# Three transfers in flight instead of two in the scatter of tokens into expert slots

## The chip, the cores and the metric

The kernel runs on one core of one Trainium2 chip. The metric is the time of one execution on the device in microseconds. One execution was also recorded by the hardware profiler; its span and its rows are those shown here.

## The reference

One adaLN transformer block for x of shape (4, 512, 256): modulated layer norm, attention with low-rank q and k/v and a rotary part, then modulated layer norm and a mixture of experts. The part that matters here is the mixture of experts. Each of the 2048 tokens goes to 4 of 16 experts:

```python
weights, indices = _gate(xt, gate_w)              # top 4 of 16, from the best 2 of 4 groups
combine = jnp.einsum('tk,tke->te', weights, one_hot(indices, E))
h1 = jnp.einsum('td,eid->tei', xt, W1)
h3 = jnp.einsum('td,eid->tei', xt, W3)
g = silu(h1) * h3 * combine[:, :, None]
y = jnp.einsum('tei,edi->td', g, W2)
z = silu(xt @ Ws1.T) * (xt @ Ws3.T) @ Ws2.T        # shared experts, all tokens
x = x + gb * (y + z)
```

## The kernel before

The work comes in stages. A first stage makes modulations, norms and weights. Attention follows, 64 heads over 256 units, and takes the span up to about 670 us. At its end the second layer norm and the gate's logits are made for the last batch entry.

VectorE then chooses the four experts of every token and computes a slot for each of the 2048 x 4 pairs of token and expert (`places`). Slots are grouped by expert, in 80 tiles of 128 slots (`SLOT_TILES`), padded where an expert's number of tokens is no multiple of 128. Its last step writes `slot_i` and raises `indexed`.

From there two things run side by side. TensorE, VectorE and ScalarE do the two shared experts, 16 positions of one token tile each (`shared_position`); between them VectorE forms the low parts of the routed weights. GpSimd scatters: for each of 16 token tiles and each of 4 ranks, an indirect DMA takes the 128 rows of the tile from SBUF (`h2`, 288 float32 each: 256 values, 16 weights, 16 destinations; 147 KB) and writes them to the DRAM tensor `slots`, each row at its slot number. These are 64 scatters, in the loop over `t` and `r`, line 1913. Before each one but the first two, GpSimd waits until the scatter two before it has landed. Two semaphores, `sent[0]` and `sent[1]`, count the even and the odd scatters by 16.

SyncE waits for `indexed`, starts one weight load (`w2_s`, experts 8 to 12), waits for `listed`, and then for both `sent` semaphores at their final counts:

```python
sp.wait_ge(listed, 1)
for z in range(IN_FLIGHT):
    sp.wait_ge(sent[z], landed(NT * TOPK, z))
sp.wait_ge(z_x, NT)
```

`landed(k, z)` is 16 times the number of scatters among the first k on semaphore z. Only then does SyncE load slot tiles, in order, up to three ahead of the tile being computed (`load_slots`). The routed experts run over these 80 tiles on TensorE, VectorE and ScalarE (`expert_position`), and after each tile GpSimd scatters its 128 result rows to their places in `parts` (line 1926). That loop allows up to four of its scatters in flight, by the four semaphores `e_put`. A last stage adds four parts for each token.

`IN_FLIGHT` is used nowhere else than in the list of semaphores, in `landed`, in SyncE's wait above and in the scatter.

Of the kernel before, what the change touches and what calls it, by code (L numbers as in the profile page):

```python
# [40 lines left out]
NT = NB * TB  # L41
# [7 lines left out]
E, TOPK, EG, TOPG = 16, 4, 4, 2  # L49
# [9 lines left out]
XW = D + 2 * E  # L59
NOWHERE = NT * P * TOPK  # L60
PARTS_AHEAD = 8
IN_FLIGHT = 2
CYCLE = 4
PACK = CYCLE + 2
assert SLOT_TILES % CYCLE == 0 and E ** PACK <= 2 ** 24
# [69 lines left out]
def program(nc, x, cT, wmod, wdn, wqup, wkup, wvup, wout, wrope, trig, eye, qnw_bc, kvw, kvw2, wgate, w13, w2,  # L135
            route, out):
    ctx = ExitStack()
    with ctx:
        def sb(name, shape, dt=F32):
            return ctx.enter_context(nc.sbuf_tensor(name, shape, dt))  # L140

        def sem(name):
            return ctx.enter_context(nc.semaphore(name))
# [6 lines left out]
        slots = nc.dram_tensor("slots", [SLOT_TILES * P, XW], F32).ap()  # L150
# [18 lines left out]
        slot_i = sb("slot_i", [P, NT, TOPK], U32)  # L169
# [139 lines left out]
        h2 = sb("h2", [P, NT, XW])  # L309
# [20 lines left out]
        def rows_of(b):  # L330
# [48 lines left out]
            ("padded", "pad_set", "masked", "listed", "indexed", "extended"))  # L379
        sent = [sem(f"sent{j}") for j in range(IN_FLIGHT)]  # L380

# [83 lines left out]
        def landed(k, z):  # L465

            return 16 * ((k + IN_FLIGHT - 1 - z) // IN_FLIGHT)

# [22 lines left out]
        def _(sp):  # L491
# [131 lines left out]
# [3 lines that stand above are left out]
# [33 lines left out]
        def _(pe):  # L659
# [95 lines left out]
            def aux(t):  # L755
                dst = aux_home(t)
                if AUX_K[t] >= 2:
                    pe.wait_ge(*read_out(AUX_LIST[AUX_K[t] - 2]))
                if t[0] == "pr":
                    _, w, r = t  # L760
                    b, g = r // PAIRS, r % PAIRS
                    if b > 0 and g == 0 and w == 0:
# [11 lines left out]
                elif t[0] == "ht":  # L774
                    _, b, k = t
                    pe.wait_ge(f_xn, b + 1)
                    for q in range(TB):
                        mm = pe.transpose(dst[:, q * P:(q + 1) * P], stage[:, q, k * P:(k + 1) * P], ident[:])
                elif t[0] == "lg":
                    mm = logits(dst[:, 0:TB * E], t[1])  # L780
                elif t[0] == "bt":
                    mm = turn_back(dst, t[2])
                elif t[0] == "ot":
                    p = t[1]

                    pe.wait_ge(s_norm, 2 * p + 2)
                    for q in range(TB):
                        mm = pe.transpose(dst[:, q * P:(q + 1) * P], o_tok[:, p % 2, q, :], ident[:])
                else:
                    _, g, n = t  # L790
                    if n == 0:
                        pe.wait_ge(s_ol, 2 * g + 2)
                    g2 = 2 * g % PAIRS
                    for q in range(2):
                        for pp in range(2):
                            tok = slice((2 * n + q) * P, (2 * n + q + 1) * P)
                            mm = mm3(dst[:, q * D:(q + 1) * D], oT[:, pp, 0, tok], oT[:, pp, 1, tok],
                                     mout[:, 0, g2 + pp, :],
                                     mout[:, 1, g2 + pp, :], pp == 0, pp == 1)
# [985 lines left out]
        def _(pool):  # L1785
# [119 lines left out]
            pool.wait_ge(f_h2, 2 * NB)  # L1905
            pool.wait_ge(extended, 2)
            pool.wait_ge(indexed, 1)
            for t in range(NT):
                for r in range(TOPK):
                    z, landed = r % IN_FLIGHT, (t * TOPK + r) // IN_FLIGHT  # L1910
                    if landed > 0:
                        pool.wait_ge(sent[z], 16 * landed)
                    pool.indirect_dma_start(slots, bass.IndirectOffsetOnAxis(ap=slot_i[:, t, r:r + 1], axis=0),  # L1913
                                            h2[:, t, :], None).then_inc(sent[z], 16)

            last_part = pool.to_reg(NOWHERE - 1)

# [99 lines left out]
```

## Time and profile before

| | us |
|---|---|
| timed executions | 1052.15, 1061.2, 1081.17 |
| median | 1061.2 |
| profiled execution, whole | 1050.47 |
| its span in the trace | 1048.7 |
| TensorE busy | 870.9 (83%) |
| VectorE busy | 733.7 (70%) |
| GpSimd busy | 666.4 (64%) |
| ScalarE busy | 568.5 (54%) |
| GpSimd, 64 scatters into `slots`, busy | 64.2 |
| idle time of GpSimd just before them | 60.3 |

Busy shares are means over stages with different limits, so they don't say what bounds one stage. In the rows, PE is TensorE, PEld its weight loads, DVE VectorE, ACT ScalarE, POOL GpSimd and SP SyncE; L1913 is line 1913 of the kernel. A GpSimd DMA instruction's time is that of the instruction on the engine; its landing is the time from the instruction's start to the moment when all its data has arrived and its semaphore has its full count. The chain that ended last is followed back from the last instruction, at each step to what released it; "issue" in it is time in which nothing that the profile shows was waited for. PEclk is TensorE's granted clock as a share of 2.4 GHz.

### The profile page before, as it was taken

The page shows a single profiled execution, that of the slowest core. Times are in us where ns is not written, and L with a number is a line of the kernel's source. Part 1 is how long each engine was busy: PE and PEld are TensorE (multiplying, and loading weights), DVE is VectorE, ACT ScalarE, POOL GpSimd, SP SyncE. Part 2 cuts the span into 40 slices and gives each one's busy share as a digit, 9 for nine tenths or more (in the row PEclk, how much of TensorE's full clock was granted, in tenths as well). Part 3 has the DMA queues.
Part 4 walks back from the last instruction along what each step waited for, and adds up shares of the span by engine and source line. Part 5 has one row for each costly group of instructions (what it writes and reads, how often), then busy time and mean ns, then how long its engine had stood idle before and what let it go on. Part 6 is the DMA issues. An engine that isn't in the chain of part 4 may idle for free.

```text
span 1048.7 us, 19959 instructions
## 1 busy us (share of the span) xinstructions
PE 870.9 (83%) x6996; PEld 740.5 (71%) x6996; DVE 733.7 (70%) x1648; ACT 568.5 (54%) x1062; POOL 666.4 (64%) x641
## 2 busy tenths in 40 slices
PE   4563799999999999999999997737990899999920
PEld 4552477888878888788888786637880798998920
DVE  5674676878788787978788885586880466666656
ACT  1201387878778788887887886522320344444410
POOL 3513378888888878797888885504666255555544
PEclk9776799999999999999999999857995899999965
DMA  5654243223432233422325135233222333333254
GB/s 183 227 189 95 44 138 80 79 60 68 117 103 58 68 82 84 145 54 74 86 56 159 40 99 211 81 78 92 97 101 108 106 116 110 122 119 119 88 217 184
DMA packets 66332, 113.69 MB, mean 108 GB/s; under 512 B 16981, under 2 KB 43484, under 8 KB 64268
## 3 DMA queue, kind: packets, MB, share of 16 engines
q1 hardware_dynamic: 47337, 71.21, 25.7%
q10 hardware_dynamic: 11987, 23.36, 6.3%
q0 software_dynamic: 6912, 17.84, 4.4%
q8 instruction: 59, 0.97, 0.4%
q14 instruction: 37, 0.30, 0.1%
HBM read 46.45 MB, written 41.68 MB: 84 GB/s over the span
## 4 chain that ended last, share of the span: by engine, by line
PE 59%; DVE 12%; DMA 12%; POOL 7%; issue 5%; ACT 3%; SPq 0%; POOLq 0%; DVEq 0%; ACTq 0%
PE bank L661 13%; PE bank L663 11%; PE bank L662 11%; DMA slots<-h,slot_i 8%; PE bank L834 7%; PE bank L1038 6%; PE bank L811 4%; POOL p_lo L1858 3%; POOL turns L1836 2%; PE bank L1010 2%; PE bank L897 2%; DVE turns L1197 1%; DVE turns L1198 1%; DVE h L1545 1%; DMA rows_f<-turns 1%
## 5 line engine op out<-in xcount | busy, mean ns | idle before, releaser
L1858 POOL TENSOR_TENSOR p_lo<-p_f,p_hi 128x512 f16<-128x512 f32 x256 | 324.5, 1279 | 62.2 <-ACT p_f L1602 61.7
L1224 DVE TENSOR_REDUCE nmax<-bank 128x1 fp32r<-128x512 f32 x256 | 174.3, 686 | 98.1 <-PE bank L811 94.3
L1599 ACT ACTIVATE p_hi<-bank,log_up 128x512 f16<-128x512 f32 x256 | 176.2, 688 | 110.4 <-PE bank L663 101.2
L1602 ACT ACTIVATE p_f<-bank,log_up 128x512 f32<-128x512 f32 x256 | 175.4, 685 | 6.8 <-POOL p_lo L1858 6.8
L834 PEld LDWEIGHTS bank<-vals,p_hi 128*128 128x128 f16 x2048 | 110.4, 98 | 51.3 <-issue 23.6
L834 PE MATMUL bank<-vals,p_hi 128*128 128x66 f16 x2048 | 138.7, 194 | 7.6 <-POOL p_lo L1858 7.0
L661 PE MATMUL bank<-qk 128*128 128x512 f32 x256 | 122.6, 479 | 8.2 <-issue 7.8
L1204 DVE TENSOR_TENSOR qk<-rows_f,qk 128x512 fp32r<-128x512 f32 (+1 forms) x128 | 127.4, 995 | 2.0
L1836 POOL TENSOR_TENSOR turns<-turns 128x512 f32<-128x512 f32 x64 | 89.3, 1398 | 55.1 <-DVE turns L1198 55.1
L834 PE MATMUL bank<-vals,p_lo 128*128 128x66 f16 x1024 | 121.1, 193 | 0.0
L811 PE MATMUL bank<-qk 128*128 128x512 f32 x256 | 103.4, 407 | 6.1 <-DVE nmax L1224 4.0
L1913 POOL DMA_INDIRECT slots<-h,slot_i x64 | 64.2, 1004 | 60.3 <-DMA slots<-h,slot_i 29.6
L663 PE MATMUL bank<-qk 128*128 128x512 f32 x256 | 102.4, 400 | 0.0
L662 PE MATMUL bank<-qk 128*128 128x512 f32 x256 | 101.1, 395 | 0.0
L834 PEld LDWEIGHTS bank<-vals,p_lo 128*128 128x128 f16 x1024 | 96.4, 97 | 0.5
L811 PEld LDWEIGHTS bank<-qk 128*128 128x128 f32 x256 | 79.3, 310 | 19.7 <-DVE nmax L1224 5.1
L1926 POOL DMA_INDIRECT parts<-h,sel_i x80 | 79.7, 997 | 13.2 <-POOL idle L1925 11.7
L1038 PE MATMUL bank<-w_p,gT 88*128 x320 | 82.7, 381 | 0.4 <-DVE gT L1531 0.3
L1591 ACT ACTIVATE qk<-rows_f 128x512 fp32r<-128x512 f32 (+1 forms) x128 | 80.5, 629 | 1.6
L1925 POOL TENSOR_TENSOR idle<-mhalf 128x1 f32<-128x1 f32 x80 | 14.9, 186 | 86.0 <-ACT h L1779 85.9
L1779 ACT ACTIVATE h<-bank 128x256 f32<-128x256 f32 x80 | 30.8, 385 | 62.7 <-PE bank L1038 62.7
L661 PE MATMUL bank<-h_st,wr_hi 128*128 128x512 f32 x128 | 52.5, 410 | 11.5 <-issue 7.3
(231 smaller groups left out, 2106.1 us busy)
## 6 DMA issues: line engine op xcount, KB each, us to landing
rows_f<-turns SPq DMA_DIRECT2D x64, 256.0 KB, 3.9
slots<-pad ACTq DMA_DIRECT2D x4, 2880.0 KB, 10.2
h<-slots SPq DMA_DIRECT2D x80, 144.0 KB, 2.1
w_hi<-parts SPq DMA_DIRECT2D x16, 512.0 KB, 7.8
rows_f<-kl_f SPq DMA_DIRECT2D x32, 192.0 KB, 3.0
w_raw<-in_w ACTq DMA_DIRECT2D x4, 1408.0 KB, 12.1
h_dram<-h_hl SPq DMA_DIRECT2D x3, 1024.0 KB, 4.8
qk<-lat_st SPq DMA_DIRECT2D x16, 192.0 KB, 4.2
```

Source lines behind the costliest of these rows:

```text
L661: pe.matmul(dst, l_hi, r_hi, start=start, stop=False)
L662: pe.matmul(dst, l_hi, r_lo, start=False, stop=False)
L663: return pe.matmul(dst, l_lo, r_hi, start=False, stop=stop)
L811: pe.matmul(max_bank[q % 2][:], qk[:, s % RING, 0, 0, :].rearrange("k (p t) -> k t p", t=TB)[:, q, :], qk[:, s % RING, 1, 0, :], start=Tru ...
L834: mm = pe.matmul(out_bank[s % 2][:, q * VW:(q + 1) * VW], p[:, c, tok], vals[:, s // H * TB + c, a, :], start=(c == 0 and q == 0 and n == ...
L1038: mm = pe.matmul(y_bank[j % 2][:, 0:D], gT[:, j % 2, 0, h, :], w2_s[:, bass.ds(expert, 1), h, :].rearrange("p a n -> p (a n)"), start=(h = ...
L1204: dve.tensor_tensor(qk[rows, s % RING, x, 1, :], rows_f[rows, (s // 2) % 2, x, s % 2, :], qk[rows, s % RING, x, 0, :].bitcast(F32), ALU.su ...
L1224: dve.tensor_reduce(nmax[:, k % MAXES:k % MAXES + 1], max_bank[q % 2][:], AX_X, ALU.max, negate=True)\
L1599: act.activation(p_hi[:, u % TB, :], score_bank[u % 2][:], ACT.Exp, bias=log_up[:, 0:1], scale=SCALE)
L1602: act.activation(p_f[:, u % 2, :], score_bank[u % 2][:], ACT.Exp, bias=log_up[:, 0:1], scale=SCALE)\
L1836: pool.tensor_tensor(turns[:, 0, w], turns[:, 0, w], turns[:, 1, w], ALU.add if w else ALU.subtract).then_inc(s_eo, 1)
L1858: pool.tensor_tensor(p_lo[:, u % TB, :], p_f[:, u % 2, :], p_hi[:, u % TB, :], ALU.subtract).then_inc(s_pl, 1)
```

## The change

Three semaphores instead of two. The scatters are numbered k = 0 to 63 in the same order as before. Scatter k uses semaphore k mod 3 and, from k = 3 on, waits until scatter k - 3 has landed. SyncE waits for three semaphores (counts 22, 21 and 21 times 16) instead of two.

```diff
-IN_FLIGHT = 2
+IN_FLIGHT = 3
...
-            for t in range(NT):
-                for r in range(TOPK):
-                    z, landed = r % IN_FLIGHT, (t * TOPK + r) // IN_FLIGHT
-                    if landed > 0:
-                        pool.wait_ge(sent[z], 16 * landed)
-                    pool.indirect_dma_start(slots, bass.IndirectOffsetOnAxis(ap=slot_i[:, t, r:r + 1], axis=0),
-                                            h2[:, t, :], None).then_inc(sent[z], 16)
+            for k in range(NT * TOPK):
+                t, r = k // TOPK, k % TOPK
+                if k >= IN_FLIGHT:
+                    pool.wait_ge(sent[k % IN_FLIGHT], 16 * (k // IN_FLIGHT))
+                pool.indirect_dma_start(slots, bass.IndirectOffsetOnAxis(ap=slot_i[:, t, r:r + 1], axis=0),
+                                        h2[:, t, :], None).then_inc(sent[k % IN_FLIGHT], 16)
```

## Rows read from the trace of the kernel before

**Rows 1.** Chain that ended last, shares of the span by engine and line.

```profile
PE bank L661 13%; PE bank L663 11%; PE bank L662 11%; DMA slots<-h,slot_i 8%; PE bank L834 7%; PE bank L1038 6%; PE bank L811 4%; POOL p_lo L1858 3%; POOL turns L1836 2%; PE bank L1010 2%; PE bank L897 2%; DVE turns L1197 1%; DVE turns L1198 1%; DVE h L1545 1%; DMA rows_f<-turns 1%
```

**Rows 2.** The chain in order of time: start us, us, what.

```profile
714.56 7.12 DMA slots<-h,slot_i
721.68 0.27 issue
...
754.87 3.67 DMA slots<-h,slot_i
...
772.99 4.32 DMA slots<-h,slot_i
...
810.75 2.45 DMA slots<-h,slot_i
813.33 2.10 DMA h<-slots
815.48 0.70 PE bank L1010 x2
```

**Rows 3.** Timeline, end of the shared experts: start us, us, instruction, idle before.

```profile
784.73 2.83 PE L938 MATMUL bank<-w_p,gT 88*128 88x256 f32 x12
...
788.74 0.42 DVE L1467 TENSOR_TENSOR xa<-xa,zg 128x256 f32<-128x256 f32 x1
```

**Rows 4.** Stretches: length, busy us by engine (instructions), PEclk, DMA share, GB/s.

```profile
790.00:800.00 10.00, 0.00 (x0) 0.00 (x0) 0.00 (x0) 0.00 (x0) 6.83 (x8) 0.56 0.27 106
800.00:810.00 10.00, 0.00 (x0) 0.00 (x0) 0.00 (x0) 0.00 (x0) 7.30 (x8) 0.50 0.30 115
```

**Rows 5.** SyncE's waits: us in total, times, longest us.

```profile
SPq L625 <- DMA slots<-h,slot_i: 99.2, 1, 99.2
```

**Rows 6.** Timeline of GpSimd, the scatter: start us, us, instruction, idle before.

```profile
714.56 1.22 POOL L1913 DMA_INDIRECT slots<-h,slot_i  x1 [27.45 <-DVE slot_i L1408]
716.09 0.96 POOL L1913 DMA_INDIRECT slots<-h,slot_i  x1 [0.30 <-issue]
721.94 0.96 POOL L1913 DMA_INDIRECT slots<-h,slot_i  x1 [4.89 <-DMA slots<-h,slot_i]
723.21 0.96 POOL L1913 DMA_INDIRECT slots<-h,slot_i  x1 [0.30 <-issue]
...
806.59 0.96 POOL L1913 DMA_INDIRECT slots<-h,slot_i  x1 [0.30 <-DMA slots<-h,slot_i]
808.04 0.96 POOL L1913 DMA_INDIRECT slots<-h,slot_i  x1 [0.49 <-DMA slots<-h,slot_i]
```

**Rows 7.** The scatter's line: duration ns min/median/max; what ended the idle before; landing.

```profile
L1913 POOL DMA_INDIRECT slots<-h,slot_i x64: 955/961/1607, 714.6 to 810.8; - x64
...
  DMA slots<-h,slot_i: 29.6, 52
...
DMA to landing us min/median/max: 2.4/2.5/7.1
```

**Rows 8.** TensorE's granted clock by short stretches, columns as in rows 4.

```profile
792.00:793.00 1.00, 0.00 (x0) 0.00 (x0) 0.00 (x0) 0.00 (x0) 0.71 (x1) 0.50 0.19 74
...
822.00:823.00 1.00, 1.00 (x8) 1.00 (x7) 1.00 (x5) 0.38 (x1) 0.00 (x0) 1.00 0.06 21
```

**Rows 9.** Two single scatters: the instruction with its start, and its transfer's landing.

```profile
L1913 POOL DMA_INDIRECT slots<-h,slot_i x1: 959/959/959, 756.3 to 756.3; - x1
...
DMA to landing us min/median/max: 2.6/2.6/2.6
...
L1913 POOL DMA_INDIRECT slots<-h,slot_i x1: 959/959/959, 774.4 to 774.4; - x1
...
DMA to landing us min/median/max: 3.3/3.3/3.3
```

**Rows 10.** The scatter into parts: its line, and its first transfer in the chain.

```profile
L1926 POOL DMA_INDIRECT parts<-h,sel_i x80: 995/997/1013, 825.1 to 1004.6; - x80
...
825.14 4.72 DMA parts<-h,sel_i
```

## Prediction

> **What bounds the kernel now.** I read the chain that ended last first. Its summary gives 8% of the span to the scatter's transfers, `slots<-h,slot_i` [rows 1]; only matrix multiplications take more. The reader should then look at the chain in order of time [rows 2]: from 714.56 to 813.20 us it is nothing but scatter, a transfer of about 2.4 us, 0.27 us of issue, the next transfer. Before it stands VectorE's slot computation, behind it SyncE's first load of a slot tile, which starts at 813.33, and TensorE's first transpose of that tile at 815.48.
>
> Is anything else late at that moment? TensorE's last work of the shared experts starts at 784.73 and lasts 2.83 us, VectorE ends at 789.16 [rows 3]. The table of stretches shows TensorE with no instruction at all from 790 to 810, while GpSimd runs 8 scatters in each 10 us [rows 4]. SyncE waited 99.2 us in one wait for the scatter [rows 5]. So the end of the scatter alone starts the routed experts, and whatever it gains up to about 24 us (813.2 less 789.2) reaches the end, since all 80 tiles are queued behind that load.
>
> What bounds the scatter itself? GpSimd's own timeline [rows 6]: an instruction takes 0.96 us, and where nothing is waited for the next one starts 0.30 us later, a pitch of 1.26 us. The pause of 0.30 stands even before the second instruction, which has no wait in the code, so it isn't the wait's cost. The transfer lands 2.4 to 2.5 us after the start of its instruction (median, [rows 7]). With two in flight, instruction k+2 can start 2.44 + 0.27 = 2.71 us after instruction k. GpSimd alone would need 2.52 for the two. That is the pattern of the last rows: starts 1.45 and 1.26 apart in turn.
>
> **The change part by part.** The third semaphore moves each wait from the transfer two back to the one three back. The number of instructions and bytes stays: 64 scatters of 128 rows. One semaphore is added, the waits on GpSimd go from 62 to 61, and SyncE gets a third wait beside two, all on counts reached at the same moment; I put these at 0.05 us each and so at nothing. GpSimd has only the 64 scatters queued behind the waiting instruction, then the routed experts' steps, which need the loads anyway.
>
> *First stall.* The first transfer lands at 714.56 + 7.12 = 721.68 [rows 2], beside a weight load issued at 713.67. Now scatter 2 (counted from 0) waits for it and scatter 3 follows at 723.21. With three, scatter 2 goes out at 717.35 (716.09 + 0.96 + 0.30) and scatter 3 is the one that waits, until 721.68 + 0.27 = 721.95. Gain 1.26 us; the stall itself stays, since the landing sets it.
>
> *The steady part.* From the start of scatter 3 (723.21) to that of scatter 63 (810.75) are 87.54 us in 60 steps. The instructions' durations in it add up to 60.1 us (the 64.2 of all, less 4.1 for the first three and the last): 60 x 0.96 = 57.6, and the rest in a dozen instructions of up to 1.61 us [rows 7]. The fixed pauses are 60 x 0.30 = 18.0. What remains, 87.54 - 78.1 = 9.4 us, is waiting for landings. With three in flight scatter k+3 can start 2.71 us after scatter k, while GpSimd's own three steps take 3 x 1.26 = 3.78. The wait is met 1.07 us before it is asked, so the steady waiting goes. Late landings stay where they exceed that slack: the one of 4.32 us (started 772.99, [rows 2]) allows the third scatter behind it after 4.32 + 0.27 = 4.59, against 3.8 of own steps, and leaves 0.8. The one of 3.67 (started 754.87) needs 3.94 against 1.26 + 1.26 + 1.49 = 4.0 with its longer neighbour, and leaves nothing. Gain 9.4 - 0.8 = 8.6 us.
>
> *Sum.* 1.3 + 8.6 = 9.9 us. The scatter would end at 803.3 instead of 813.2, still 14 us behind VectorE's last work: next late is the scatter again, now bound by GpSimd's 64 instructions. Behind it nothing depends on absolute time. TensorE's granted clock is 1.00 until 791, 0.60 in the next microsecond and 0.50 from 792 on [rows 8]; its last matmul ended at 787.6. It restarts at 815.48 at 0.50 and has 1.00 from 822. With the scatter ending at 803.3 TensorE restarts at 805.5, after 18 us of idling instead of 28, and by the same rows at 0.50 too; I take the slow start as unchanged.
>
> *Bounds of what the trace doesn't show: three in flight.* The landing of each could grow. I replayed the 64 scatters with their own durations and landings; with two in flight the replay ends at 813.4 (the trace: 813.2), with three at 803.3. With every landing 1.0 us longer the three end at 807, with 1.5 us longer at 815, no gain. I take no lengthening, because of the nearest rows: where a late transfer made them bunch, the transfers started at 754.9 and 756.3 landed after 3.7 and 2.6 us, at 758.6 and 758.9; those started at 773.0 and 774.4 after 4.3 and 3.3, at 777.3 and 777.7 [rows 9]. Two landings 0.3 to 0.4 us apart say that the transfers need far less than 1.26 us each of the engines that move them; so does the DMA share of 0.27 to 0.30 in these stretches [rows 4], some 0.35 us per transfer. On the other side the stretched instructions (2.8 us in all above 0.96) could vanish, which would make the gain 12.7.
>
> The row says 2.44 us from start to landing. The Trainium skill, DMA: Bandwidth & Descriptors, section on the anatomy of one DMA, gives a GpSimd-issued DMA some 2.0 us fixed plus its bytes over 436 GB/s. My estimate from that page is 2.34 us for 147 KB, so two in flight would allow a pitch of (2.34 + 0.27)/2 = 1.31 against 1.26, and the steady gain without late landings would be 3 us, by the measured row (1.355 against 1.26) 5.7. The row is used.
>
> **Against the median.** The profiled execution took 1050.47 us, its span 1048.7 and 1.8 around it; minus 9.9 is 1040.6. The three timed ones are 1052.15, 1061.2 and 1081.17: the profiled one is the fastest of four. From the middle of the four (1056.7) the change gives 1046.8; from the median of three 1051.3. I forecast 1047. A measurement of this kernel can tell about 2% (21 us) from no change, so the forecast, -0.9%, is "within 2%".
>
> **The rivals.**
> *Landings serve in turn.* If the completion of the scatters is the bottleneck, one every 1.35 us, a third in flight only waits longer: every landing grows by 1.36 us, the pitch stays, and only the 1.3 us of the first stall is won: 1049 on the profiled execution, 1055 by the middle of four. For it: every step of the chain is a transfer. Against it: landings 0.3 to 0.4 apart. 10%.
> *Slower: the third overloads the queue.* Place: the 60 steady steps. From a landing of 1.36 us more, 3.8 in all, the three in flight are slower than the two. Rows with such landings exist: the first scatter's 7.12 us beside a load, and the first scatter into `parts`, 4.72 us [rows 10]. At 4.72 the pitch is (4.72 + 0.27)/3 = 1.66, at 7.12 it is 2.46; against 87.54/60 = 1.46 that costs 12 or 60 us: 1063 to 1110 on the profiled execution. The same price comes if GpSimd has no room for a third's descriptors and stands inside its instruction. Against: the scatters into `parts` are 80 with up to four in flight by the code, and their instructions take 995 to 1013 ns, none stretched [rows 10]. As an estimate from the Trainium skill's descriptor size and count per engine (the same page, 16 B and 9 a side), three transfers take 432 B a side and engine, little beside the 16 KiB of descriptor scratch that SBUF — State Buffer, section on SBUF size, names; no run here shows either. 4%.
> *More than forecast.* The stretched instructions shrink or the late landings don't recur: 12 to 13 us, 1044 by the middle of four. 10%.
> *The change does nothing for the end,* because the shared experts end last: they would have to end 14 us later than in the trace. 1%.
>
> **How the numbers follow.** My forecast, a gain of 8 to 12 us, has 75%. Range: the low end is the profiled execution with the largest gain, 1050.5 - 12.7 = 1038; the high end the median of three with no gain and a little, 1064. It leaves out the slow rival and medians outside these executions. Faster by over 2% would need 21 us, more than the 14 that an unbounded number in flight gives in the replay (ended at 799.2), so it is left to the spread of the timings: 5%. Slower by over 2%: 4%, from the second rival and the spread. Within: 91%.
>
> **What would show it.** Right: scatter starts 1.26 to 1.27 apart, GpSimd's pauses before them 0.30 and put to issue, waiting for `slots` down from 29.6 us to about 5; the scatter's last start near 801; the first `h<-slots` near 803.4; TensorE idle some 18 us; landings still 2.4 to 2.5. Wrong: landings of 3.5 us or more in the steady part with the pitch still 1.35 (first rival), instructions over 1.2 us in the quiet stretch behind 790 (no room), or a clock that comes back later than 7 us after the restart.

## The result and the profile after

The changed kernel took 1090.7 us (median of five, 1089.0 to 1097.2) against 1061.2 us (1051.5 to 1081.2) for the kernel before: a ratio of 1.038, with a 95% interval of 1.034 to 1.042. The ratio compares fast executions alone and so leaves out two of the kernel before, at 1078.5 and 1081.2 us, which were over 1.5% above its fastest; the two plain medians give 1.028. That was one set of executions. The experiments below ran the changed kernel in three more sets, each on a chip of its own: 1.039 in one of them, 0.993 and 0.991 in the other two. So this section reads an execution in which the change did harm, and the experiments show that it isn't the whole answer.

First the page of the profiled execution (1097.15 us): its span and the chain's shares by engine. Beside [rows 1], the scatter's 8% is gone, and 7% stand under a name that the chain before didn't have.

```profile
span 1095.3 us, 19959 instructions
...
PE 62%; DVE 12%; another core or an unknown queue 7%; POOL 6%; issue 4%; DMA 3%; ACT 3%; SPq 0%; POOLq 0%; DVEq 0%; ACTq 0%
```

The scatter's own line. Beside [rows 7] the wait for a landing fell from 29.6 us in 52 pauses to 4.3 in one, and 62 pauses are put to issue.

```profile
L1912 POOL DMA_INDIRECT slots<-h,slot_i x64: 957/962/1326, 713.3 to 797.8; - x64
...
  DVE slot_i L1408: 27.5, 1
  issue: 18.9, 62
  DMA slots<-h,slot_i: 4.3, 1
```

GpSimd's timeline, the steady start and the end of the scatter, beside [rows 6]: starts 1.26 to 1.27 us apart.

```profile
721.43 0.96 POOL L1912 DMA_INDIRECT slots<-h,slot_i  x1 [4.35 <-DMA slots<-h,slot_i]
722.70 0.96 POOL L1912 DMA_INDIRECT slots<-h,slot_i  x1 [0.30 <-issue]
723.96 0.96 POOL L1912 DMA_INDIRECT slots<-h,slot_i  x1 [0.30 <-issue]
...
796.53 0.96 POOL L1912 DMA_INDIRECT slots<-h,slot_i  x1 [0.30 <-issue]
797.80 0.96 POOL L1912 DMA_INDIRECT slots<-h,slot_i  x1 [0.30 <-issue]
```

Scatter 3 to scatter 63 took 797.80 - 721.43 = 76.4 us where they took 87.5. The scatter did what was forecast, and more. The time was lost elsewhere. SyncE's waits (total, times, longest), beside [rows 5]:

```profile
SPq L625 <- DMA slots<-h,slot_i: 86.2, 1, 86.2
SPq L626 <- PE bank L947: 47.4, 1, 47.4
```

The wait for the scatter is 13 us shorter, but a wait of 47.4 us for TensorE follows it, in the next line of the code (`z_x`, the shared experts' last transpose). In the table of stretches, with columns as in [rows 4], the shared experts stand nearly still while GpSimd scatters, and run at full rate after it. The first row is from the trace of before, the others from the trace after:

```profile
760.00:770.00 10.00, 9.40 (x57) 8.46 (x55) 8.08 (x22) 3.85 (x10) 7.08 (x7) 1.00 0.27 104
```

```profile
760.00:770.00 10.00, 0.00 (x0) 0.00 (x0) 1.56 (x3) 0.00 (x0) 7.56 (x9) 0.50 0.31 118
...
780.00:790.00 10.00, 0.00 (x0) 0.00 (x0) 0.00 (x0) 0.32 (x1) 7.68 (x8) 0.50 0.30 118
...
800.00:810.00 10.00, 1.83 (x6) 1.83 (x7) 2.55 (x6) 1.48 (x4) 0.00 (x0) 0.51 0.00 0
...
820.00:830.00 10.00, 10.00 (x63) 9.21 (x62) 7.63 (x19) 3.79 (x10) 0.00 (x0) 1.00 0.01 2
```

In the stretches shown from 760 and 780 us TensorE has no record at all; in the trace of before it was busy for 9.4 and 7.6 of their 10 us, and had only the end of the shared experts left in the second. The DMA share is 0.30 and 0.31 in the stretches with the scatter, little more than the 0.27 to 0.30 of [rows 4], and next to nothing moved in the two after it. In the chain in order of time (start us, us, what) these are the long pieces:

```profile
735.20 14.02 another core or an unknown queue
749.46 0.78 ACT w_hi L1628
750.24 20.71 another core or an unknown queue
770.99 16.05 another core or an unknown queue
787.09 20.29 another core or an unknown queue
807.41 0.33 ACT sl L1750
...
861.32 0.42 PE bank L1010 x2
```

"Another core or an unknown queue" means that the profile found no instruction whose end fits the moment at which the waiting engine was released. The way to read it is to pair the waits by hand. The n-th `sl` activation of ScalarE waits for the n-th group of TensorE's inner products, whose last matmul has line 663. The timeline of the three engines shows two such pairs, the fifth and the eleventh, and a signal in the other direction:

```profile
721.00 0.32 PE L663 MATMUL bank<-ws_hi,x_hl 128*128 128x352 f32 x1
...
739.73 0.49 PE L663 MATMUL bank<-ws_hi,x_hl 128*128 128x352 f32 x1
...
721.36 0.32 ACT L1750 ACTIVATE sl<-bank 128x176 f32<-128x176 f32 x1 [0.58 <-PE bank L663]
...
787.07 0.32 ACT L1750 ACTIVATE sl<-bank 128x176 f32<-128x176 f32 x1 [15.71 <-remote]
...
753.82 0.33 DVE L1449 TENSOR_TENSOR g_s<-bank,sl 128x176 f32<-128x176 f32 x1
...
754.20 0.66 PE L661 MATMUL bank<-ws_hi,x_hl 128*128 128x352 f32 x1 [11.87 <-DVE g_s L1449]
```

The fifth group ends at 721.00 + 0.32 and ScalarE starts at 721.36, 0.04 us later. The eleventh ends at 739.73 + 0.49 = 740.22 by its record, and ScalarE starts at 787.07, 46.9 us later. The whole list, in us: 0.03 to 0.04 for the first seven, then 1.0, 5.2, 17.2, 46.9, 51.1 and 13.0, and 0.03 to 0.05 from the fourteenth on, which comes at 810. The same pairing in the trace of before gives 0.04 for all 32. VectorE's signal to TensorE was in time: `g_s` ended at 753.82 + 0.33 and TensorE started at 754.20.

The other consumers of TensorE's results show the same, with up to 52 us for `gT`. So signals from TensorE came late, and the one shown in the other direction did not. The trace also records the semaphore that ScalarE waits for, and its eleventh step stands at 787.05, just before ScalarE starts: the delay lies before the semaphore, not behind it. A record's end on TensorE is modelled, so the trace can't say whether the matmuls themselves finished late or only their signals left late. It does say that they came in order, at about the rate of the matmuls: after `gT` at 753.48 VectorE's `zg` came at 764.67 (four matmuls further, 11.2 us), ScalarE's `x_hl` at 770.97 (two, 6.3), `sl` at 787.07 (six, 16.1) and `gT` at 792.67 (two, 5.6). That is 2.7 to 3.2 us for each matmul, where one takes 0.2 to 0.5 in its record. It ended at 807.4, 9.6 us behind the start of the last scatter, and the backlog was gone by 810. TensorE began the routed experts at 861.32 instead of 815.48, 45.8 us later; the span grew by 46.6.

### The profile page after: what moved, and what is told of

It is laid out like the page before. It is cut to its first block, busy times and chain, and to the rows that moved or that the text cites. A ratio compares the mean times of both kernels' runs of the same rounds, so it can differ in the third digit from the quotient of the medians.

```text
span 1095.3 us, 19959 instructions
## 1 busy us (share of the span) xinstructions
PE 882.1 (81%) x6996; PEld 748.3 (68%) x6996; DVE 734.0 (67%) x1648; ACT 569.2 (52%) x1062; POOL 664.2 (61%) x641
## 4 chain that ended last, share of the span: by engine, by line
PE 62%; DVE 12%; another core or an unknown queue 7%; POOL 6%; issue 4%; DMA 3%; ACT 3%; SPq 0%; POOLq 0%; DVEq 0%; ACTq 0%
PE bank L661 13%; PE bank L663 11%; PE bank L662 11%; PE bank L834 7%; PE bank L1038 6%; PE bank L811 4%; POOL p_lo L1858 3%; PE bank L897 2%; PE bank L938 2%; POOL turns L1836 2%; PE bank L1010 2%; DVE turns L1197 1%; DVE turns L1198 1%; DMA rows_f<-turns 1%
## 5 line engine op out<-in xcount | busy, mean ns | idle before, releaser
L661 PE MATMUL bank<-ws_hi,x_hl 128*128 128x352 f32 x64 | 28.0, 437 | 72.4 <-issue 34.6
L661 PEld LDWEIGHTS bank<-ws_hi,x_hl 128*128 128x128 f32 x64 | 14.2, 222 | 75.8 <-issue 40.4
```

Source lines behind the costliest of these rows:

```text
L661: pe.matmul(dst, l_hi, r_hi, start=start, stop=False)
```

## The experiments

Each set ran on one chip, together with the kernel before, and ratios are to that. The chips of the sets B to G are six different ones. The first measurement is called chip A here; which chip it was isn't known, so it may be one of the six. Each set also ran at a time of its own, so where the text says "chip", it means a chip together with its moment: nothing here tells the two apart.

### Set on chip B: what in the scatter delays TensorE's signals

**Three semaphores, two in flight.**

```diff
-                if k >= IN_FLIGHT:
-                    pool.wait_ge(sent[k % IN_FLIGHT], 16 * (k // IN_FLIGHT))
+                if k >= 2:
+                    pool.wait_ge(sent[(k - 2) % IN_FLIGHT], 16 * ((k - 2) // IN_FLIGHT + 1))
```

> Three semaphores in turn, but each scatter still waits for the one two before it, so that only two are in flight. In the trace of the changed kernel the scatter ran as forecast (last start 797.8 us), but signals from TensorE to ScalarE and VectorE came 4 to 36 us late while it ran. Theory A (a scatter stream that GpSimd never has to hold back for a landing delays TensorE's signals): this kernel holds back as before, so it is the kernel before, within 0.5%, with waits of 29 us on the scatter and no late signals. Rival B (the third semaphore, SyncE's third wait or their numbering does it): some 3.8% slower, as the changed kernel.

Measured: 1.0017 (0.9988 to 1.0045), 1051.5 us. The third semaphore costs nothing that shows. The pairing of `sl` shows delays of 0.5 to 2.8 us on six signals, so on this chip two in flight, at 1.50 us per scatter at mean, were already not quite free of it.

**A small addition before each scatter.**

```diff
+                pool.wait_ge(pool_c, own[0])
+                own[0] += 1
+                pool.tensor_tensor(idle[:, 1:2], mhalf[:, 0:1], mhalf[:, 0:1], ALU.add).then_inc(pool_c, 1)
                 pool.indirect_dma_start(slots, ...
...
+            pool.wait_ge(pool_c, own[0])
```

> Three in flight, and a small GpSimd addition of 0.19 us before every scatter, so that GpSimd never waits for a landing but starts a scatter only every 1.6 us. Theory A1 (what hurts is the pace of 1.26 us): no late signals, scatter 61 x 0.35 us longer than the changed kernel's, ending near 821, so some 0.8% slower than the kernel before. Rival A2 (what hurts is that GpSimd never stands at a semaphore, whatever its pace): late signals stay, shared experts end far behind 810, slower by 3% or more. Rival A3 (three transfers in flight at once hurt): at 1.6 us a landing of 2.45 leaves two in flight at most, so this agrees with A1.

Measured: 1.000 (0.998 to 1.002), 1050.0 us. GpSimd's timeline shows that I had mis-sized the pause: the addition takes the place of the fixed 0.30 us, so the pitch is 1.38, not 1.6.

```profile
718.00 0.18 POOL L1914 TENSOR_TENSOR idle<-mhalf 128x1 f32<-128x1 f32 x1 [3.38 <-DMA slots<-h,slot_i]
718.34 0.99 POOL L1915 DMA_INDIRECT slots<-h,slot_i  x1 [0.15 <-POOL idle L1914]
...
719.72 0.99 POOL L1915 DMA_INDIRECT slots<-h,slot_i  x1 [0.16 <-POOL idle L1914]
```

The waits by engine (total us, times, longest) show waits for late signals of at most 2.6 us; the pairing gives up to 3.3 us, on 12 of the 32 `sl`:

```profile
ACT sl L1750 <- remote: 6.9, 4, 2.6
...
DVE zg L1464 <- remote: 2.9, 2, 1.4
```

GpSimd never stood at a scatter's semaphore in the steady part, and the harm stayed small; that speaks for the pace and against rival A2. With the instructions that were stretched, the mean step was 1.49 us, that of the kernel with two in flight beside it 1.50.

**The addition before every fourth.** The same three lines stand under `if k % 4 == 3:`.

> Three in flight, the small GpSimd addition only before every fourth scatter: mean pitch near 1.35 us, as in the kernel before, but in runs of four scatters at 1.26 us with nothing waited for. Theory A1 with a threshold in the mean pace between 1.26 and 1.36 us: no late signals and the time of the kernel before, within 1%. Rival A2 (never waiting hurts): late signals and 3% slower. If the threshold lies in single runs of 1.26 us, some late signals of a few us, and a time between the two.

Measured: 1.039 (1.032 to 1.046), 1089.1 us, with starts 1.27 to 1.35 apart, 1.30 at mean over the first group of four in the steady part. TensorE's signals are late through most of the scatter again, by the pairing up to 30 us:

```profile
ACT sl L1750 <- remote: 42.2, 9, 12.3
DVE gT L1457 <- remote: 41.8, 8, 12.7
```

So on this chip starts 1.30 us apart did the full harm and starts 1.38 us apart little. These are the steps without stretched instructions; over all 60 steady steps the means are 1.36 and 1.49 us. The mean step of the kernel before, 1.46 us, which this kernel was meant to come near, was missed.

**Every eighth waits for the one before.**

```diff
+                if k % 8 == 7:
+                    pool.wait_ge(sent[(k - 1) % IN_FLIGHT], 16 * ((k - 1) // IN_FLIGHT + 1))
```

> Three in flight, but every eighth scatter waits for the one right before it, so that the stream empties seven times: each time about 1.4 us, some 11 us in all, so the scatter alone would end near 811. Theory A as a backlog (the delay of TensorE's signals grows over many scatters, from 4 us to 36, and is worked off in a pause): late signals of a few us at most, time within 1% of the kernel before. Rival (any run of unhindered scatters delays signals at once): late signals of more than 5 us remain and it is 2% or more slower.

Measured: 1.008 (1.003 to 1.012), 1059.0 us. By the pairing `sl` comes up to 1.9 us late and `zg` up to 3.3, none by tens of us, though seven of eight steps wait for no landing: that fits a backlog that needs a stretch of scatters to grow and that a pause of 2.2 us works off. The pauses themselves put the scatter's last start at 817.9 us.

### Set on chip C: a finer pace, half the bytes

**The addition before every second; half rows, three in flight; the addition before the first 48; half rows, two in flight.** The conditions are `k % 2 == 1` and `k < 48`; the half rows are `h2[:, t, 0:XW // 2]`, written to a tensor of its own:

```diff
-                pool.indirect_dma_start(slots, bass.IndirectOffsetOnAxis(...), h2[:, t, :], None)
+                pool.indirect_dma_start(slots_half, bass.IndirectOffsetOnAxis(...), h2[:, t, 0:XW // 2], None)
```

> Three in flight, the small GpSimd addition before every second scatter. Measured so far: addition before every scatter, pitch 1.38 us, time of the kernel before; before every fourth, mean pitch 1.30, 3.9% slower. The pitch here should be 1.32. Theory (the scatters load something that TensorE's signals need, and it keeps up to a pace of one scatter in some 1.30 to 1.38 us): in between, signals late by 1 to 10 us, shared experts end before or a little behind the scatter, time 0 to 2% over the kernel before. Rival (any stream without waiting delays them and the addition alone helps by its own slot): as with every fourth, 3 to 4% slower.

> Leaves out half of the data: each scatter writes 144 of the 288 columns, into a tensor that nobody reads, three in flight; the routed experts compute on the padding alone, and their rows go nowhere (parts is zeroed in attention, 8 MB of extra transfers there). If bytes are the load that delays TensorE's signals, the pace of 1.26 us now carries half of them and no signal is late: shared experts end some 75 us after slot_i, as in the kernel before. If the number of transfers and of their descriptors is the load, the signals are as late as in the changed kernel, and the shared experts end 120 us or more after slot_i.

> Three in flight, the small addition before each of the first 48 scatters only, so pitch 1.38 us while the shared experts run and 1.27 for the last 16, when TensorE has nothing to do. Theory of the pace: signals in time, and the last 16 save 16 x 0.11 = 1.8 us against the addition before all (1050.0 us): 1048, 0.998 of the kernel before. Rival (anything at the pace of 1.26 us harms, also with TensorE idle): no gain or a loss of a few us.

> Leaves out the same half of the data as the half-row kernel with three in flight, but keeps two in flight. The landing should shorten by 0.2 us or so from 2.45, which brings the two-deep pitch from 1.355 to 1.26 to 1.30. If the number of transfers matters and the pace alone sets it, signals are late here too, with only two in flight. If three in flight is what hurts, none is late.

Measured: every second 0.999 (0.998 to 1.001); until 48 0.997 (0.996 to 0.999); the half rows 1059.6 and 1062.6 us with the extra work that they carry. None of the four shows a late signal: every pair of `sl` is at 0.04 us. For the half rows with three in flight this looked like the answer that bytes are the load. It wasn't one, since the control came in the next set.

### Set on chip D: the control

**Wide rows with the addition; full rows into another tensor; two in flight until scatter 24; every second until 48.** The wide rows take 384 columns from `h2_flat`; the third has `back = 2 if k < 24 else 3` and waits for scatter k - back.

> Each scatter takes 384 columns instead of 288 (a third more bytes; the extra ones are the neighbouring tile's) and writes them into a tensor that nobody reads; the routed experts compute on the padding alone. The small GpSimd addition stands before every scatter, so the pitch is 1.38 us or more, a pace at which 288 columns did no harm. If bytes per us are the load that delays TensorE's signals, these 142 GB/s are more than the 117 GB/s of the changed kernel, and signals are late by 10 us and more. If the pace of scatters is the load, no signal is late.

> The control of the half-row kernels: full 288 columns at the full pace, three in flight, but into a tensor that nobody reads, with the same zeroing of parts in attention; the routed experts compute on the padding alone. If the half rows were what kept the signals in time, they are late here as in the changed kernel (TensorE's shared experts end 120 us or more after the scatter's start). If the other tensor or the zeroing did it, none is late here and the half-row result says nothing on bytes.

> Two in flight for the first 24 scatters, three afterwards. If the late signals grow out of the full pace at any time while the shared experts run, they begin near scatter 24 (750 us) and the kernel is 1.5 to 3% slower than before. If it takes the start of the scatter (the burst of three behind the 7 us landing, beside the weight load) to set them off, none is late, the scatter ends near 807, and the time is 0.995 of the kernel before.

> Three in flight, the small addition before every second one of the first 48 scatters, none after. Before every scatter until 48 gave 0.997, before every second of all gave 0.999 without late signals in its trace. If the pace with every second is safe, the stage is as in that kernel and the tail saves 8 additions of 0.06 us at mean: 0.999 or a little less. If it is near the edge, some executions carry late signals and the times spread up to 1060.

Measured: 1065.8 us for the wide rows and 1056.9 for the full rows into another tensor, both with their extra work; 0.995 (0.993 to 0.998) for two until 24, and 0.996 (0.995 to 0.998) for every second until 48. Again no late signal in any. The control is the surprise: full rows, full pace, three in flight, and nothing late.

```profile
L1915 POOL DMA_INDIRECT slots_other<-h,slot_i x64: 956/960/1487, 728.6 to 818.5; - x64
...
  issue: 18.0, 59
```

That took away every conclusion from chips C and D about what the load is. What set them apart from A and B had to be the other tensor, the start of the scatter, or the chip and its moment, and the changed kernel itself had run on neither.

### Sets on chips E, F and G: the changed kernel again

**The changed kernel, unedited, beside one with two in flight for the first four scatters** (chip E; `back = 2 if k < 4 else 3`).

> The changed kernel once more, as a control. Full rows at the full pace of 1.26 us gave no late signal in two later kernels (full rows into another tensor, and three in flight from scatter 24 on), which both ran on another chip than the ones that showed late signals. Theory C (the late signals hang on the chip): on a chip like those, this kernel has none, its scatter ends 10 us earlier and it takes 0.990 to 0.995 of the kernel before. Rival D (they hang on the start of the scatter, three at once beside the weight load): as in the first measurement, 1.038.

> Two in flight for the first four scatters only, three from then on: it takes away the third scatter beside the weight load and leaves the full pace. Rival D (the start sets the late signals off): none here, 0.990 to 0.995, whatever the changed kernel does beside it. Theory C (the chip decides): the same as the changed kernel beside it on the same chip, within 0.3%: about 0.991 on a chip without late signals, 1.03 or more on a chip with them.

Measured: 0.993 (0.990 to 0.995), 1043.6 us, and 0.992 (0.990 to 0.995), 1043.9 us. The kernel that had been 3.8% slower is 0.7% faster here. Its scatter line and the end of its chain:

```profile
L1912 POOL DMA_INDIRECT slots<-h,slot_i x64: 956/960/1782, 713.8 to 804.4; - x64
...
  issue: 18.0, 59
  DMA slots<-h,slot_i: 6.2, 4
...
DMA to landing us min/median/max: 2.4/2.5/6.7
```

```profile
772.30 4.08 DMA slots<-h,slot_i
...
804.43 2.43 DMA slots<-h,slot_i
806.92 2.04 DMA h<-slots
```

TensorE ended the shared experts at 786.9 and began the routed ones at 809.0, with the clock at its lower level from 792 us on and at the restart:

```profile
792.00:808.00 16.00, 0.00 (x0) 0.00 (x0) 0.00 (x0) 0.00 (x0) 10.35 (x11) 0.50 0.29 112
808.00:812.00 4.00, 2.59 (x8) 1.80 (x9) 1.32 (x6) 0.77 (x2) 0.00 (x0) 0.50 0.65 188
```

**The changed kernel a third time, and the half rows beside it** (chip F).

> The changed kernel a third time. On the first chip it took 1.038 of the kernel before with TensorE's signals up to 50 us late; on a second chip 0.993 with none late. Theory C (the chip decides): either 0.990 to 0.995 with none late, or 1.03 to 1.04 with signals late, and nothing between, the same in all executions on one chip. Rival F (chance from execution to execution, or from load to load): executions of both kinds in one set.

> Leaves out half of each scattered row (144 of 288 columns, into a tensor nobody reads; the routed experts compute on the padding alone, parts is zeroed in attention). Beside the changed kernel on the same chip: if that one has late signals, this tells whether bytes matter: none late here if bytes per us are the load, late by tens of us if the number of transfers is. If the changed kernel has none late, this has none either and tells nothing new.

Measured: 1.039 (1.029 to 1.048), 1095.8 us, all four executions between 1089 and 1099. Here the chip is of the first kind, and the half rows had late signals too, up to 54 us by the pairing (1113.4 us with their extra work):

```profile
L1915 POOL DMA_INDIRECT slots_half<-h,slot_i x64: 957/962/1222, 731.6 to 815.3; - x64
...
  issue: 18.9, 62
```

```profile
ACT sl L1753 <- remote: 53.1, 3, 33.3
DVE gT L1458 <- remote: 52.5, 2, 33.7
```

They carry half the bytes at the same pace, into another tensor, so halving the bytes per us doesn't take the delay away, and the tensor `slots` isn't needed for it. That rests on a single execution. It leaves what goes with the number of scatters per us: their instructions, their rows, their landings.

**The changed kernel a fourth time, and the addition until 48** (chip G).

> The changed kernel a fourth time, as the marker of the chip: 1.03 to 1.04 of the kernel before with late signals on a chip that has them, 0.990 to 0.995 on one that has not.

> Three in flight with the small addition before each of the first 48 scatters, 0.997 on a chip without late signals. If this is a chip with late signals (the changed kernel beside it tells), the pace of 1.38 us should keep them below 3 us each, as the addition before every scatter did on such a chip, and the time at 0.995 to 1.000; if it doesn't, 1.02 or more. On a chip without them, 0.997 again.

Measured: 0.991 (0.988 to 0.993), 1040.7 us, and 0.995 (0.994 to 0.997), 1045.0 us, nothing late in either. The end of the changed kernel's chain here:

```profile
767.78 4.03 DMA slots<-h,slot_i
...
799.93 2.42 DMA slots<-h,slot_i
802.41 2.20 DMA h<-slots
```

Chip G doesn't have the late signals, so whether the addition until 48 holds on one that has stays open; only the addition before every scatter was measured on such a chip.

**What the sets say together.** The changed kernel ran in four sets: slower by 3.8 and 3.9% on A and F, in nine executions of nine, faster by 0.7 and 0.9% on E and G, in six of six. Rival F named two chances. Chance from execution to execution predicted mixed sets and falls. Chance from load to load isn't excluded: in the sets D, E and F two kernels at the full pace ran side by side, and each time both did the same, which speaks for the set and against the load, but three pairs are few. Rival D (the start of the scatter) falls with the changed kernel on E and G, which has that start. Large delays need both a chip that is prone to them and a fast pace: on chip B 1.38 us between scatters did little, 1.30 did the full harm. The pace alone doesn't decide: on E and G the changed kernel's mean step was 1.37 us, about that of the harmful kernel on B (1.36), and nothing was late. The kernel before runs at 1.46 at mean. On the prone chips A and F single executions of it took 1078 to 1082 us, on C, D, E and G none of 55 took over 1054, but on the prone chip B none of 20 did either. The long ones fit a two-deep kernel that now and then gets too fast, but no trace of such an execution exists.

**What else goes with the late signals: lost records.** The profiler should record 16 steps of a semaphore for each of the 64 landings, 1024 in all. The trace of before and all twelve traces of the sets C, D, E and G hold 1022 to 1024 of them. The trace of the changed kernel on A holds 174, the two on F 180 and 176, the four on B, in the order above, 565, 507, 212 and 596. These seven are the traces with late signals; the four with 212 records or fewer have `sl` late by 30 to 56 us, the three with more by 1.9 to 3.3. The view of the DMAs shows it too: it gives the scatter's landing in the trace of before (first line) and can't in the trace after (second).

```profile
slots<-h,slot_i POOLq DMA_INDIRECT x64, 2.5
```

```profile
slots<-h,slot_i POOLq DMA_INDIRECT x64
```

On A the records are whole for the first three landings and go missing from the fourth on, at about 724 us, before the first late signal. On B, in the three kernels with small delays, they are whole again from 792 us on, when the shared experts have ended. So a rival stands untested: on these chips the recording itself can't keep up with the events, and it is what holds TensorE back. Half rows cause as many events, so it fits them too. Each timed execution here has a span and a granted clock beside its time, so none is known to have run without a recording, and the loss of 3.8% may not exist where nothing is recorded.

There is also a part that feeds itself. While VectorE works, some of GpSimd's scatter instructions are stretched (to 1.2 to 1.8 us, about every fourth), which lowers the pace. Once TensorE's signals are late, VectorE idles, and the stretches go: after 726.8 us the changed kernel on chip A shows no instruction over 0.97 us. That would explain why it doesn't recover before the scatter ends. It is read from the traces and wasn't tried by itself.

**Open.** What the scatter and TensorE share on the prone chips, and what sets those chips, or those moments, apart. Whether TensorE finished late or only signalled late. Whether the recording causes the delay, or both come of the same thing. The cause of the loss is shown only so far: TensorE's signals come late while the scatter runs dense.

## Why the prediction was wrong

It was wrong on chip A and on chip F. On E and G the times, 1043.6 and 1040.7 us, lie in its range. Step by step:

- *What bounds the kernel.* Right. The end of the scatter starts the routed experts; on chips E and G all that it gained reached the end.
- *First stall.* Right: on E scatter 3 started 0.27 us behind the first landing.
- *The steady part,* forecast 78.9 us from scatter 3 to 63 instead of 87.5. On chip A 76.4, since hardly an instruction was stretched. On E 804.4 - 722.0 = 82.4, and here a term was mis-sized: fourteen instructions were stretched by 5.7 us in all, where I had kept the 2.5 of before and bounded them only downwards. Late landings such as the one of 4.08 us cost 1.0 beyond the fixed pauses, where 0.8 was forecast. The gain of the whole was 7.3 us on E and 9.8 on G (medians), against 9.9 forecast.
- *Three in flight lengthen the landing.* Bounded at 0 to 1.5 us, taken as 0. Right: 2.4 to 2.5 us on E and G. On A and F the traces have no landing times; GpSimd's steps of 1.27 us with nothing waited for say that nearly all were over within three of them, 3.8 us. At a pitch of 1.265 a landing of 2.45 is over before the second next starts, so apart from the few late landings the steady part never has three transfers under way; the third semaphore only spares GpSimd the 0.27 us between a landing and its next start.
- *The clock.* Right: 0.50 through the idle time and at the restart on E.
- *"Next late is the scatter again".* This is the step that failed. The prediction left the end of the scatter 14 us of room behind the shared experts and took the time of their end over from the trace of before. On chips A and F they ended 70 us later, SyncE waited 47.4 us for TensorE behind the scatter, and the routed experts began on A at 861.32 us instead of the forecast 805.5. What the runs show in its place is TensorE's signals up to 52 us late (A) while the scatter ran; why they are late stays open. I priced the change by GpSimd, the transfers and their landings, and held the other engines' traces constant; nothing in it asked what a denser stream of GpSimd's DMAs does to engines that share no semaphore and no data with it.
- *The rivals.* The slower one had its place (the steady part) and in 1063 to 1110 us its price right, but by luck: its mechanism was a scatter slowed by landings over 3.8 us or by longer instructions, and the scatter on A was faster than forecast, 1.27 us per step at mean with the median instruction at 0.96. "The shared experts end last" was among the rivals, at 1%, for a gain of nothing: the right consequence, without a reason that could bring it about, and the weight that such a rival gets.
- *The range* took its upper end from the spread of the kernel before. Two of the five executions of it on chip A, 1078 and 1081, may have been the same effect at work; no trace shows it.
- *The page.* An estimate from the Trainium skill (DMA: Bandwidth & Descriptors, section on the anatomy of one DMA) gave 2.34 us for a transfer where the row had 2.44; with half the bytes, on chip C, the landing was 2.3 us where the same formula gives an estimate of 2.17. It changed nothing.

## What to carry to other kernels

A wait that looks like pure loss can be what holds an engine at a pace that the rest of the core bears, and the trace of before needn't show it. When a change makes one engine issue DMAs faster, look in the trace after at the other engines' waits, "remote" or "unknown queue" above all, and pair the n-th signal with the n-th wait. Count the records of such a trace as well: where many are missing, the recording may be part of what it shows. And repeat a surprising ratio on another chip before explaining it: here the same kernel gave 0.991 and 1.039, and two sets of experiments without the changed kernel in them were nearly read as an answer on bytes. The variants with an addition before each or every second scatter gave 0.995 to 1.000 where they ran; they give up half of the gain or more, and the only one of them measured on a prone chip, with all 64 paced, kept clear of the loss. The addition before every fourth did not: 1.039.

## What the runs showed of the hardware

- In two of four sets (and in a third with a near variant), under recording, TensorE's signals to ScalarE came up to 51 (A) and 56 us (F) late while GpSimd scattered 128 rows every 1.27 us, on A at about 2.8 us per matmul. The signal of VectorE to TensorE that was read came in time. With half the bytes per row they were up to 54 us late (F, one execution).
- The traces with late signals hold 174 to 596 of the 1024 records of the scatters' landings, all others, that of before on chip A among them, 1022 to 1024.
- On one such chip (B) starts 1.38 us apart brought delays of up to 3.3 us, starts 1.30 us apart of up to 30.
- Between two scatters on GpSimd pass 0.30 us with nothing waited for. An addition of 0.18 us between them brings this to 0.16 + 0.18 + 0.15, and the scatter itself takes 0.99 instead of 0.96: it costs 0.11 us of pitch.
